# Who makes the key differences for the pair maxima: VectorE and ScalarE from PSUM, or GpSimd from SBUF

## What is computed

```
out = bilinear_resize(x, H // 2, W // 2)
out = relu(bn(conv1x1(out, conv1_w), bn1_s, bn1_b))
q = conv1x1(out, q_w, q_b).reshape(B, -1, N)      # 32 channels, N = 4096
k = conv1x1(out, k_w, k_b).reshape(B, -1, N)      # 32 channels
v = conv1x1(out, v_w, v_b).reshape(B, C, N)       # 256 channels
attn = softmax(einsum('bdi,bdj->bij', q, k), axis=-1)
out = gamma * einsum('bcj,bij->bci', v, attn) + out
out = relu(bn(out, bn2_s, bn2_b))
out = bn(conv1x1(out, conv2_w), bn3_s, bn3_b)
return relu(bilinear_resize(out, H, W) + x)
```

## Time and profile before

| what | value |
|---|---|
| median of 3 runs | 2516.56 us (2513.71 to 2520.03) |
| the profiled execution | 2517.04 us, its span 2515.2 us |
| TensorE busy | 2304.0 us, 92% |
| VectorE busy | 1845.6 us, 73% |
| ScalarE busy | 1807.3 us, 72% |
| GpSimd busy | 1603.2 us, 64% |

### The profile page before, as it was taken

One profiled execution on the slowest core, in us unless ns is written; L12 is line 12 of the kernel. 1 busy time (PEld: TensorE's weight loads), 2 busy tenths in 40 slices (PEclk: granted clock), 3 DMA queues, 4 the chain that ended last, 5 costly groups with the idle time before them and its releaser, 6 DMA issues.

```text
span 2515.2 us, 48184 instructions
## 1 busy us (share of the span) xinstructions
PE 2304.0 (92%) x15914; PEld 1640.0 (65%) x15914; DVE 1845.6 (73%) x3403; ACT 1807.3 (72%) x3361; POOL 1603.2 (64%) x1537
## 2 busy tenths in 40 slices
PE   4699999999989999999989999999999999999981
PEld 2277777777467777777737777777746777777760
DVE  7856577776777777777686777777676777777779
ACT  5457777777547777887747788877754778877862
POOL 7870088888328888888824888888840444444475
PEclk8999999999999999999999999999999999999995
DMA  6330022222102222222201222222300111111133
GB/s 208 109 93 1 1 76 100 100 93 105 46 26 84 101 100 101 100 92 100 102 17 43 101 101 100 101 100 98 111 26 12 67 66 67 60 66 67 67 101 134
DMA packets 59129, 204.11 MB, mean 81 GB/s; under 512 B 8736, under 2 KB 9824, under 8 KB 58976
## 3 DMA queue, kind: packets, MB, share of 16 engines
q1 hardware_dynamic: 40544, 135.26, 16.8%
q10 hardware_dynamic: 18432, 67.12, 6.5%
HBM read 135.24 MB, written 67.11 MB: 80 GB/s over the span
## 4 chain that ended last, share of the span: by engine, by line
PE 71%; DVE 18%; issue 5%; ACT 4%; DMA 1%; SPq 1%; POOL 1%; DVEq 0%; ACTq 0%; POOLq 0%
PE acc L1056 14%; PE acc L1058 14%; PE acc L1057 14%; PE et L934 8%; PE emx L922 5%; PE wrk L954 4%; PE acc L982 4%; DVE xres L725 4%; DVE xres L722 3%; DVE pl L695 2%; PE wrk L922 2%; ACT above L434 2%; PE acc L974 2%; DVE mx L667 1%; PE wrk L946 1%
## 5 line engine op out<-in xcount | busy, mean ns | idle before, releaser
L1056 PE MATMUL acc<-vh,ph 128*128 128x257 f16 x4096 | 1120.7, 274 | 21.5 <-DVE pl L695 20.1
L1058 PE MATMUL acc<-vh,pl 128*128 128x257 f16 x4096 | 1116.4, 273 | 0.0
L1057 PE MATMUL acc<-vl,ph 128*128 128x256 f16 x4096 | 1111.1, 271 | 0.0
L695 DVE TENSOR_TENSOR pl<-et,ph 128x512 f16<-128x512 f32 x1024 | 702.2, 686 | 140.1 <-ACT et L426 135.8
L425 ACT ACTIVATE ph<-et 128x512 f16<-128x512 f32 x1024 | 610.2, 596 | 259.3 <-PE et L934 256.2
L426 ACT ACTIVATE et<-et 128x512 f32<-128x512 f32 x1024 | 609.1, 595 | 0.0
L1057 PEld LDWEIGHTS acc<-vl,ph 128*128 128x128 f16 x4096 | 401.0, 98 | 274.8 <-issue 20.5
L1056 PEld LDWEIGHTS acc<-vh,ph 128*128 128x128 f16 x4096 | 400.3, 98 | 95.5 <-DVE pl L695 26.7
L1058 PEld LDWEIGHTS acc<-vh,pl 128*128 128x128 f16 x4096 | 395.5, 97 | 56.2
L934 PE MATMUL et<-qs,ks 98*128 (+1 forms) x1024 | 390.3, 381 | 30.4 <-DVE pl L695 30.3
L335 POOL TENSOR_TENSOR rd<-win 128x320 f32<-128x320 f32 x124 | 119.4, 963 | 443.1 <-ACT win L457 343.0
(11 more groups left out here) (130 smaller groups left out, 2826.5 us busy)
## 6 DMA issues: line engine op xcount, KB each, us to landing
xres<-in_x SPq DMA_DIRECT2D x146, 512.0 KB, 4.5
out<-xres ACTq DMA_DIRECT2D x128, 512.0 KB, 2.6
xin<-in_x SPq DMA_DIRECT2D x110, 512.0 KB, 3.7
osb<-in_L_conv_conv_w SPq DMA_DIRECT2D x1, 256.0 KB, 7.5
osb<-in_L_conv_v_w SPq DMA_DIRECT2D x1, 256.0 KB, 7.5
hbuf<-in_L_conv_conv_w SPq DMA_DIRECT2D x1, 256.0 KB, 7.4
ident<-identity SPq DMA_DIRECT2D x1, 64.0 KB, 7.6
uw<-up_weights SPq DMA_DIRECT2D x1, 64.0 KB, 2.5
```

The costliest lines, as they stand in the source:

```text
L695: ops.tensor_tensor(pl[:, t % 4, :], et[t % 2][:, :], ph[:, t % 4, :], ALU.subtract).then_inc(pl_rdy, 1)
L1056: mm(acc[it][:, 0:C + 1], ph[:, tt % 4, pt], vh[:, tt, 0:C + 1], start=tt == 0, stop=False)
L1057: mm(acc[it][:, 0:C], ph[:, tt % 4, pt], vl[:, tt, :], start=False, stop=False)
L1058: last = mm(acc[it][:, 0:C + 1], pl[:, tt % 4, pt], vh[:, tt, 0:C + 1], start=False, stop=tt == JT - 1)
```

## The change

GpSimd makes the differences. Once the low parts of an odd chunk are done it subtracts all 96 rows of the two chunks in one instruction (L388; this gives the two copies of the high part of the difference, and in between rows that are overwritten later), subtracts high rows and low rows into float32 `k_hi` and `k_lo` (L389, L391), takes from `k_hi` what the half-precision result already holds (L393), and adds the rest to the low part (L395). All operands lie in SBUF. VectorE's four instructions for an odd chunk, ScalarE's copy for an even one and its wait on `qk_done` go. The four pairs stand at the head of GpSimd's `enter`, in all four images.

```
+            def key_differences(b, m):
+                even, odd = (slice(c * IB, (c + 1) * IB) for c in (2 * m, 2 * m + 1))
+                ds = slice(m * IB, (m + 1) * IB)
+                done = (b * JP + m) * 4
+                pool.wait_ge(qk_done, b * NB + 2 * m + 2)
+                ops.tensor_tensor(kd[:, ds], ks[0:3 * D, odd], ks[0:3 * D, even], ALU.subtract).then_inc(kd_step, 1)
+                ops.tensor_tensor(k_hi[:, :], ks[0:D, odd], ks[0:D, even], ALU.subtract).then_inc(kd_step, 1)
+                pool.wait_ge(kd_step, done + 1)
+                ops.tensor_tensor(k_lo[:, :], ks[D:2 * D, odd], ks[D:2 * D, even], ALU.subtract).then_inc(kd_step, 1)
+                pool.wait_ge(kd_step, done + 3)
+                ops.tensor_tensor(k_hi[:, :], k_hi[:, :], kd[0:D, ds], ALU.subtract).then_inc(kd_step, 1)
+                pool.wait_ge(kd_step, done + 4)
+                ops.tensor_tensor(kd[D:2 * D, ds], k_hi[:, :], k_lo[:, :], ALU.add).then_inc(kd_rdy, 1)
+                pool.wait_ge(kd_rdy, b * JP + m + 1)
...
             def enter(b):
+                for m in range(JP):
+                    key_differences(b, m)
                 if not (isinstance(b, int) and b == B - 1):
                     pool.wait_ge(c1_rdy, b * (2 * NB) + 2 * NB)
...
                 ps = acc[bank_of("qk", ck)]
-                if ck % 2 == 0:
-                    at_least(act, qk_done, b * NB + ck)
-                    ops.copy(k_even[:, :], ps[0:2 * D, :])
                 ops.activation(ks[0:2 * D, cs], ps[0:2 * D, :], ACT.Identity, bias=qkb[0:2 * D, :])
...
                 ops.tensor_copy(ks[2 * D:3 * D, cs], ks[0:D, cs])
-                if ck % 2:
-                    ops.tensor_tensor(k_diff[:, :], ps[0:2 * D, :], k_even[:, :], ALU.subtract).then_inc(kd_step, 1)
                 for t, r in ((ks, slice(D, 2 * D)), (qs, slice(2 * D, 3 * D))):
                     last = ops.scalar_tensor_tensor(t[r, cs], ps[r, :], qkb[r, :], t[r, cs], ALU.add, ALU.subtract)
                 last.then_inc(qk_done, 1)
-                if ck % 2:
-                    m, ds = ck // 2, slice(ck // 2 * IB, (ck // 2 + 1) * IB)
-                    dve.wait_ge(kd_step, (b * JP + m) * 2 + 1)
-                    ops.tensor_copy(kd[0:2 * D, ds], k_diff[:, :]).then_inc(kd_step, 1)
-                    dve.wait_ge(kd_step, (b * JP + m) * 2 + 2)
-                    ops.tensor_copy(kd[2 * D:3 * D, ds], kd[0:D, ds])
-                    ops.tensor_tensor(kd[D:2 * D, ds], k_diff[D:2 * D, :], kd[D:2 * D, ds], ALU.subtract).then_inc(kd_rdy, 1)
```

More of the change, by code:

```diff
@@ L60, in attention_block_kernel @@
         kd = sb("kd", [3 * D, JP * IB], F16)
-        k_even = sb("k_even", [2 * D, IB])
-        k_diff = sb("k_diff", [2 * D, IB])
+        k_hi = sb("k_hi", [D, IB])
+        k_lo = sb("k_lo", [D, IB])
         above = sb("above", [P, 2, IB])
```

## The result

The changed kernel takes 2479.11 us (median of four runs, 2478.03 to 2480.09); the kernel before took 2518.27 us beside it (2513.71 to 2520.03). The ratio is 0.9846, 95% interval 0.9831 to 0.986: 39 us or 1.5% faster. The profiled execution has a span of 2476.2 us, 39.0 less than before's.

The account below looks back on a forecast made before the run. TensorE's attention was taken to hold most of the time, with VectorE's key differences on the path in the openings. Gains of 9.0 + 7.3 + 7.3 + 7.4 less 3.1 us make 27.9: 2517.0 to 2489 us, range 2480 to 2499.

Parts of the forecast that it names:

- Bound and rounds: Image openings: VectorE's chain sets the odd-to-even round; it falls from 7.78 to 6.49 us, 3.9 us an image.
- `k_even` at the first chunk: Opening of images: ScalarE's copy of chunk 0 lies on the chain; removing it gives 0.6 us.
- the other even copies: ScalarE's copies of later even chunks: removal worth nothing by itself, only keeps ScalarE from being the next to be late.
- Image 3's own term of 0.7 us: First copy of key rows in image 3: no longer slowed by GpSimd's up piece, gains 0.7 us.
- The end of the stage: End of the opening: `k_diff` 0.7 and the last `kd` stretch 2.1 go, 2.8 us; in image 3 2.2 us.
- Image 0: Opening of image 0: 6.3 us from VectorE's backlog and the end, plus 2.7 us from the clock, 9.0 us.
- GpSimd's instructions: Five new instructions a pair at 1.34 us each, 6.7 us a pair, done before TensorE needs the differences.
- the 47 us: GpSimd's time in image 0 for 20 instructions, from 102 to 149, before TensorE must wait; late-delivery rival, chance 0.04.
- the term of 3.1 us: Images 1 to 3: nine VectorE copies of high rows slowed beside a busy GpSimd, costing 3.1 us, bounds 0 to 6.1.
- 0.34 us extra: Charge for each of nine VectorE copies beside GpSimd, from seven copies averaging 0.62 us against 283 ns at best.
- The clock in images 1 to 3: The sum held a clock gain of 2.7 us for image 0 only; other images' low stretches were left to a rival.
- the clock gives more: Rival: less idle spares low-clock stretches in other images too, two more of 2.7 us, contention at nothing: 2481 us, chance 0.08.

Follow-up runs that it names:

- the run with one difference: Changed kernel with ScalarE's unused float32 copy `k_even` put back and only the first of GpSimd's five instructions per pair kept: 2485.62 us.
- The run with three times the work: Changed kernel with GpSimd's five instructions of each pair done three times over, same results: 2531.82 us.
- the run with the filled idle time: Kernel before the change with seven overwritten matmuls on TensorE ahead of its wait for the row of bounds: 2519.31 us, ratio 1.001.
- half a step later: Changed kernel with one more GpSimd instruction of 256 elements ahead of each pair's five, so they come 0.6 to 0.7 us later: 2486.4 us.
- both PSUM reads: Changed kernel with ScalarE's float32 copy `k_even` and VectorE's subtraction from PSUM `k_diff` put back, results unused: 2506.56 us.
- `k_even` alone: Changed kernel with only ScalarE's float32 copy of the even chunk put back, result unused: 2497.16 us.
- the three instructions: Changed kernel with VectorE's three half-precision instructions put back on unread scratch tiles behind each odd chunk's low parts: 2522.82 us.
- one difference: Changed kernel with only the first of GpSimd's five instructions per pair kept: 2478.79 us.
- projection first twice: Two runs: changed kernel with the last query and key projection ahead of the row of bounds, 2472.36 us; the same with unused `k_even` back, 2485.45 us.

## Where the forecast was right, and which step failed

- **Bound and rounds: right.** The six rounds from the first to the last maxima of image 1 took 704.76 - 662.06 = 42.7 us before and take 691.70 - 652.82 = 38.9: 3.8 us, against 3.9 in the sum. Both kinds are at 6.49 us.
- **`k_even` at the first chunk: right.** TensorE's wait there fell from 1.44 to 0.97 us, 0.5 against 0.6. That the other even copies are worth nothing by themselves was wrong as a statement (0.4 us a round by the run with one difference), though the term for the rounds already held it. Image 3's own term of 0.7 us is right too: its first copy takes 0.29 us, not 0.96.
- **The end of the stage: right as far as it went.** From the last maxima of the even kind to the first product with the exponentials image 1 took 38.5 us and takes 34.1, 4.4 less. The two waits that the term spoke of, 0.48 + 2.19 = 2.7 us, are gone, against 2.8. The rest, 1.7, is clock.
- **Image 0: right**, 9.0 us, clock included, within the 0.9 us by which two executions differ there.
- **GpSimd's instructions: right**, 1.22 us from start to start against 1.34, and hidden. The run with three times the work confirms both the 47 us and the way to reckon with them.
- **Contention, the term of 3.1 us: mis-sized.** The first step that failed is "0.34 us extra" for each copy, a mean of rows from another stage. A copy pays the rest of the GpSimd instruction in which it begins, 0 to about 1 us; here it began 0.1 us before the end, and the nine copies together cost 0.4 us at most. That they fell there is luck of the timing, and no merit of the design. The forecast had the copy's place almost right, 4.7 us behind the pair's start, "in its fourth instruction" (it is 663.77 - 659.17 = 4.6 us), and took from it only that there is a collision, not how much of the instruction is left: the fourth ends 4.7 us behind the start. Half a step beside it the cost is 7.4 us, some of it through the clock.
- **The clock in images 1 to 3, counted at nothing: the larger miss.** The rival "the clock gives more", 2481 us with contention at nothing, is what happened, and the forecast gave it 0.08, with the argument that "the waits ahead of the last projection stay". The wait stayed (1.58 us) and the clock rose nonetheless. The waits of the rounds before it had shrunk from 0.9 to 1.0 us down to 0.3, and the tally below says that these waits count too. I had read the clock behind one idle stretch of image 0 and not behind those of the other images, where the rows stood ready: 8.3 us.

The pieces close: 27.9 forecast + 3.1 contention not paid + 8.3 clock = 39.3 us; the spans differ by 39.0. By image 9.0, 8.5, 8.5 and 12.7 us were measured, where the terms with the clock give 9.0, 9.0, 9.0 and 12.4, so part of the closing is luck. That the clock share would be 8.3 us had the rest been left as it was isn't shown: the run with the filled idle time says that in images 1 and 2 it would have been lost again.

The thirteen traces give a tally of the low clock at the row of bounds and the last projection in images 1 to 3. Where the wait of 1.57 or 1.58 us ahead of the row stands and the rounds behind the first chunk have waits of 0.6 to 1.65 us, at least every second one (before, half a step later, both PSUM reads, `k_even` alone, `k_even` with one difference, the three instructions, three times), the low clock is there in 16 of 21 openings. Where it stands and the rounds wait 0.2 to 0.3 us (the changed kernel twice, one difference), in 1 of 9. Where it is filled or gone (the filler, projection first twice), in 0 of 9, whatever the rounds' waits. So the wait right ahead and the waits of the rounds bring it together. What stays open is in which opening: `k_even` with one difference had it in images 1 and 3 and not in 2, the half step later in image 3 alone, with the same waits in each, and one difference had it once with the waits of the changed kernel. I can't predict that from the waits alone.

## What to carry to other kernels

Before moving SBUF work to GpSimd, lay VectorE's copies over GpSimd's instructions in time: the cost of such a copy is what remains of the instruction under way, so half a step can decide over several microseconds, and SBUF work kept on VectorE at that moment can pay more than it did beside an idle GpSimd. Where TensorE's idle time shrinks, read the length of the matmuls behind every idle stretch of the kernel before; if they are at the low clock, count that too, but ask which engine will be late once TensorE isn't. And fill a wait with queued work that doesn't need it, by changing the order, before looking for anything cleverer: that gave 6.6 us here.

## What the runs showed of the hardware that I hadn't expected

- A 32 x 512 half-precision copy on VectorE takes 0.28 us alone and 0.93, 1.19 or 0.88 us when it begins 0.37, 0.22 or 0.42 us into a GpSimd instruction of 1.15 to 1.26 us; each time it ends 0.15 us after it (0.14 to 0.16 in all 159 cases). Begun 0.1 us before such an end, it still takes 0.28 us.
- It goes both ways: GpSimd instructions that take 1.14 or 1.15 us alone and begin inside VectorE's rounding to half precision, its half-precision copy or its subtraction with two SBUF inputs end 1.00 to 1.02 us behind it (42 cases), and took 1.38 us behind a rounding and 1.48 behind a subtraction.
- On GpSimd 96 partitions of half-precision inputs (1.15 us) cost the same as 32 partitions with float32 output (1.14 us), and two inputs from other partitions than the output's cost nothing extra (`k_lo` against `k_hi`, both 1.14 to 1.15 us). The fifth instruction takes 1.26 us whatever stands beside it; it has float32 inputs, half-precision output and other partitions, and which of these costs the 0.1 us no run parts.
- Filling idle time on TensorE can leave the total unchanged though the clock at that place goes to full: the low stretch came back 11 us later, 3.78 us for eight matmuls in place of 1.99.
